# Score stacks filled by SBUF-to-SBUF transfers, partner transfers issued by GpSimd

## The chip, the cores and the metric

The kernel runs on one core of a Trainium2 chip. The time is device microseconds of one execution; 924.72 us is the median of 3 runs (924.64 to 926.47).

## The reference

One layer of two blocks over x of [16, 128, 512] (batch, channel, time). The first is cross-attention over channels as rows: x is normalised over its last axis, q = Wq x + bq from it, k and v from the context, 8 heads of 16 channels, the first 8 channels of each head of q and k rotated (rotary embedding), then softmax(q k / 4) v over 512 x 512 scores per head, an output projection, and a gated sum. The second is a feed-forward block with fp4 weights.

```python
q = _proj(Wq, bq, layernorm(x)); k = _proj(Wk, bk, ctx); v = _proj(Wv, bv, ctx)
q, k = _rope(q, 8), _rope(k, 8)        # x_rope * cos + neg_half * sin on channels 0..7 of a head
p_attn = softmax(einsum('bhqd,bhkd->bhqk', q, k) / sqrt(16))
x = x + tanh(g_xattn) * _proj(Wo, bo, einsum('bhqk,bhkd->bhqd', p_attn, v))
x = x + tanh(g_ffn) * ffn(layernorm(x))
```

## The kernel before

`attend` computes the attention, `feed_forward` the second block; only the first is touched. Attention runs as 16 steps, one per batch, each of 16 slots, written out for each engine; engines meet only through semaphores, and each engine's work, SyncE's DMA issues included, is done in the order written.

In slot s of step b TensorE computes (`tensor_step`, L458): scores of batch b+1 (`score`, L412), from which VectorE takes row maxima (`maxima`, L666); scores of batch b once more, transposed, with the maxima subtracted by two more rows of the product (`weigh`, L424), which ScalarE exponentiates (L536); and the product with v for the slots before (`values`, L435). Scores have two PSUM banks, transposed results three.

The score products read *stacks*: for four pairs of heads, rows 0..47 and 64..111 hold a head's 16 channels three times, as head (rounded float32r) and rest (the remainder), in the orders head, head, rest for q and head, rest, head for k, so that one product of 48 rows gives a near-float32 result. In q's stack rows 48, 49 and 112, 113 hold the negated maxima (again head and rest), in k's ones. q and k have two stacks each, for even and odd batches.

How a stack comes about, for batch n = b+3 in step b: two projection calls (`project_rot` at slot 2, `project_pass` at slot 5), each for the q and the k of half the channels; ScalarE adds the bias; SyncE moves the rotary partners with four transfers inside SBUF (`swap_partners`, L216); GpSimd rotates (L596 to L601) and makes rests (L607, L613); VectorE casts heads (L649, L655); SyncE stores heads and rests to `image` in DRAM (L224 to L235, eight transfers of 128 or 256 KB a batch), and in the next steps loads them back into the stacks (`load_half`, L237, eight transfers of 192 KB to 48 partitions).

The maxima of a half of the slots are turned by VectorE (`turn_max`, L673), stored to DRAM (`store_max`, L249) and loaded as rows of the stack (`load_max`, L254). The weighing of slots 0 and 8 waits for them (L428). SyncE's order of a step is `sync_step` (L292), VectorE's `vector_step` (L710), GpSimd's `pool_step` (L783). Sums of exponentials are gathered (L261), halves merged (L268), inverted on VectorE at slot 6 (L684), and go through DRAM (L274, L279).

Of the kernel before, what the change touches and what calls it, by code (L numbers as in the profile page):

```python
# [17 lines left out]
P = 128  # L18
# [29 lines left out]
X_TILES, C_TILES, PROBS = 8, 4, 3  # L48
MIX_AT, ROT_AT, PASS_AT, V_AT = 1, 2, 5, 8
AHEAD_PROJ = 3  # L50

IMG_ROWS, K_ROW0 = 102, 49
STEP_ROWS = 6
# [12 lines left out]
def transposed_items():  # L66
    items = []
    for n in range(AHEAD_PROJ):
        items += [("rot", n), ("pass", n)]
    for b in range(B):  # L70
        for slot in range(SLOTS):
            items += [("weight", b, 2 * slot), ("weight", b, 2 * slot + 1)]
            if slot == MIX_AT and b >= 2:
                items.append(("mix", b - 2))
            if slot == ROT_AT and b + AHEAD_PROJ < B:
                items.append(("rot", b + AHEAD_PROJ))
            if slot == PASS_AT and b + AHEAD_PROJ < B:
                items.append(("pass", b + AHEAD_PROJ))
    items += [("mix", B - 2), ("mix", B - 1)]
    return items  # L80
# [16 lines left out]
def attend(nc, d, keep):  # L97
    with ExitStack() as ctx:
# [4 lines left out]
        halves = (slice(0, P // 2), slice(P // 2, P))  # L103
# [4 lines left out]
        scale = sb("qk_scale", [P, 1], F32)  # L108
# [12 lines left out]
        swap, turned = sb("swap", [P, T], F32), sb("turned", [P, T], F32)  # L121
        split_head = sb("split_head", [P, 2, T], F32R)
        split_rest = sb("split_rest", [P, 2, T], F32R)

        q_stack = [sb(f"q_stack{p}", [P, PAIRS, T], F32R) for p in two]
        k_stack = [sb(f"k_stack{p}", [P, PAIRS, T], F32R) for p in two]
        v_ones = [sb(f"v_ones{p}", [P, KT, QUAD, QUADS, 2 * KC], F32) for p in two]
# [29 lines left out]
        ones_set = sem("ones_set")  # L157
        gated = sem("gated")
# [17 lines left out]
        pass_head = sem("pass_head")  # L176
        pass_rest = sem("pass_rest")
        rot_head = sem("rot_head")
        rot_rest = sem("rot_rest")
        stored = [sem(f"stored_{w}") for w in ("rot", "pass")]  # L180
        half_in = [[sem(f"half_in{p}{h}") for h in two] for p in two]
# [4 lines left out]
        max_in = [[sem(f"max_in{p}{h}") for h in two] for p in two]  # L186
# [12 lines left out]
        PARTS = 16 * 4  # L199
        HALF = 16 * 4  # L200
# [3 lines left out]
        image, max_dram, inv_dram = keep["image"], keep["max_dram"], keep["inv_dram"]  # L204

        with nc.Block() as block:
# [9 lines left out]
            def swap_partners(sp, n):  # L216
                sp.wait_ge(st_read, ST_NO["rot", n] + 1)
                if n:
                    sp.wait_ge(rot_rest, n)
                for at in range(0, P, 64):  # L220
                    for to, source in ((at, at + 32), (at + 32, at)):
                        sp.dma_start(swap[to:to + 32, :], proj[source:source + 32, 0, :]).then_inc(swapped, 16)

            def store_head(sp, n, w):  # L224
                sp.wait_ge((rot_head, pass_head)[w], n + 1)
                rows = lambda first, count: image[n, first:first + STEP_ROWS * count:STEP_ROWS].rearrange("r h t -> r (h t)")
                tile = split_head[:, w, :].bitcast(F32)
                sp.dma_start(rows(3 * w + 1, 16), tile).then_inc(stored[w], 16)
                sp.dma_start(rows(3 * w, 8), tile[halves[0]]).then_inc(stored[w], 16)
                sp.dma_start(rows(K_ROW0 + 3 * w + 2, 8), tile[halves[1]]).then_inc(stored[w], 16)  # L230

            def store_rest(sp, n, w):
                sp.wait_ge((rot_rest, pass_rest)[w], n + 1)
                rows = image[n, 3 * w + 2:3 * w + 2 + STEP_ROWS * 16:STEP_ROWS].rearrange("r h t -> r (h t)")
                sp.dma_start(rows, split_rest[:, w, :].bitcast(F32)).then_inc(stored[w], 16)  # L235

            def load_half(sp, n, h):  # L237
                p = n % 2
                for w in two:
                    sp.wait_ge(stored[w], PARTS * (n + 1))  # L240
                if n >= 2:
                    sp.wait_ge(st_full, last_weight(n - 2, h))
                for stack, row0 in ((q_stack, 0), (k_stack, K_ROW0)):
                    for odd in two:
                        rows = stack[p][STACK * odd:STACK * odd + DATA_ROWS, columns(h), :].bitcast(F32)
                        heads = slice(odd * PAIRS + 2 * h, odd * PAIRS + 2 * h + 2)
                        sp.dma_start(rows, image[n, row0:row0 + DATA_ROWS, heads, :]).then_inc(half_in[p][h], 16)
# [6 lines left out]
            def load_max(sp, n, h):  # L254
                sp.wait_ge(max_out[h], 16 * (n + 1))
                for odd in two:
                    row = STACK * odd + DATA_ROWS
                    sp.dma_start(q_stack[n % 2][row:row + MAX_ROWS, columns(h), :].bitcast(F32).rearrange("r j t -> r (j t)"),
                                 max_dram[n, h, :, odd].rearrange("r i e -> r (i e)")).then_inc(max_in[n % 2][h], 16)

            def gather_sums(sp, b, h):  # L261
                sp.wait_ge(pv_out[h], b + 1)
                if b:
                    sp.wait_ge(inverse_out, 16 * QUADS * b)
                first = KC if h == 0 else 0
                sp.dma_start(sums[64 * h:64 * h + 64, :], pv_sb[h][b % 2][first:P:2 * KC, :]).then_inc(sums_in[h], 16)

            def merge_quads(sp, b):  # L268
                sp.wait_ge(sums_in[0], 16 * (b + 1))
                for j in range(QUAD):  # L270
                    rows = slice(2 * KC * j + KC, 2 * KC * (j + 1))
                    sp.dma_start(pv_sb[0][b % 2][rows, :], pv_sb[1][b % 2][rows, :]).then_inc(merged[b % 2], 16)

            def store_inverse(sp, b):  # L274
                sp.wait_ge(inverses, b + 1)
                for h in two:
                    sp.dma_start(inv_dram[b, :, h, :], sums[64 * h:64 * h + 64, :]).then_inc(inverse_out, 16)

            def load_inverse(sp, b):  # L279
                sp.wait_ge(inverse_out, 16 * QUADS * (b + 1))  # L280
                if b:
                    sp.wait_ge(heads_ok, b)
                sp.dma_start(scale_of[:], inv_dram[b].rearrange("j h t -> (j h) t").unsqueeze(1).to_broadcast(
                    [HEADS, KC, T])).then_inc(inverse_in, 16)
# [7 lines left out]
            def sync_step(sp, b):  # L292
                nxt, proj_n = b + 1 < B, b + AHEAD_PROJ
                if nxt:
                    load_half(sp, b + 1, 1)
                store_max(sp, b, 1)
                if proj_n < B:
                    swap_partners(sp, proj_n)
                if b:
                    gather_sums(sp, b - 1, 1)  # L300
                    merge_quads(sp, b - 1)
                load_max(sp, b, 1)
                if b >= 2:
                    store_x(sp, b - 2)
                if b:
                    store_inverse(sp, b - 1)
                if proj_n < B:
                    store_head(sp, proj_n, 1)
                if b + 2 < B:
                    load_half(sp, b + 2, 0)  # L310
# [4 lines left out]
                if proj_n < B:  # L315
                    store_rest(sp, proj_n, 1)
                if b + 5 < B:
                    load_inputs(sp, b + 5)
# [906 lines left out]
```

## Time and profile before

| | us |
|---|---|
| median of 3 runs | 924.72 |
| the profiled execution's own time | 918.37 |
| its span | 916.6 |
| TensorE busy | 815.8 |
| VectorE busy | 522.1 |
| ScalarE busy | 483.6 |
| GpSimd busy | 178.5 |

The span runs from the first to the last instruction of the profiled execution; its own time is 1.8 us longer, and it was 6.35 us faster than the median. Attention takes the span up to about 485 us, the feed-forward block the rest. A busy share is an average over both. PEclk is the clock that TensorE was granted, as a share of 2.4 GHz.

### The profile page before, as it was taken

What the parts mean: (1) busy time and instruction counts of PE and PEld (TensorE: products, weight loads), DVE (VectorE), ACT (ScalarE), POOL (GpSimd) and SP (SyncE); (2) the same over time, 40 slices, a digit from 0 to 9 for tenths busy, and PEclk for the clock granted to TensorE, in tenths of its full rate; (3) what the DMA queues carried; (4) which work ended last, traced back from release to release, by engine and by line L of the source; (5) the groups of instructions that cost most, each with busy time, mean ns of one, the idle gap of its engine ahead of it and who ended that gap; (6) DMA issues with size and microseconds to landing.
All of it is one profiled execution on the core that took longest, in us unless ns stands there. A gap on an engine that the chain in (4) does not pass through costs nothing. (4 is left out here: it accounts for less than half of the span.)

```text
span 916.6 us, 13653 instructions
## 1 busy us (share of the span) xinstructions
PE 815.8 (89%) x5110; PEld 421.6 (46%) x5142; DVE 522.1 (57%) x760; ACT 483.6 (53%) x895; POOL 178.5 (19%) x174
## 2 busy tenths in 40 slices
PE   3378999999998988999993599999999999999997
PEld 1123333333333333334332376666666666666664
DVE  4398977888987867888871961314131423141113
ACT  2227776887787766778792552325231623252223
POOL 1232333333333423331112820000000000000000
PEclk8559999999999988999996889999999999999999
DMA  5678555666665666465212010002000110000001
GB/s 167 171 198 218 155 142 153 189 200 194 170 165 152 175 175 189 119 167 153 69 33 79 8 46 1 1 1 67 25 1 1 47 45 0 0 27 21 0 1 46
DMA packets 55176, 86.44 MB, mean 94 GB/s; under 512 B 19274, under 2 KB 20938, under 8 KB 55114
## 3 DMA queue, kind: packets, MB, share of 16 engines
q1 hardware_dynamic: 55114, 85.62, 33.0%
q8 instruction: 38, 0.62, 0.3%
q14 instruction: 24, 0.20, 0.1%
HBM read 44.70 MB, written 34.34 MB: 86 GB/s over the span
## 5 line engine op out<-in xcount | busy, mean ns | idle before, releaser
L670 DVE TENSOR_REDUCE neg_max<-s_ps 128x2 f32<-128x1024 f32 x256 | 310.0, 1219 | 61.8 <-PE s_ps L420 60.8
L536 ACT ACTIVATE probs<-st_ps 128x512 f32<-128x512 f32 x512 | 277.9, 597 | 105.5 <-PE st_ps L432 101.2
L448 PE MATMUL pv_ps<-probs,v_ones 128*32 128x256 f32 x2048 | 166.1, 397 | 12.6 <-ACT pv_sb L542 12.6
L1098 PE MATMUL gu_ps<-x_head,gu_head 128*128 128x512 f32 x352 | 155.9, 443 | 0.0
L965 DVE TENSOR_TENSOR hidden<-gu_ps,silu 128x512 f32<-128x512 f32 x44 | 30.4, 691 | 202.6 <-ACT silu L1040 202.6
L420 PE MATMUL s_ps<-k_stack,q_stack 48*128 48x512 f32 x512 | 135.4, 526 | 10.5 <-DVE neg_max L670 8.4
L1099 PE MATMUL gu_ps<-x_rest,gu_head 128*128 128x512 f32 x352 | 139.0, 395 | 0.0
L1040 ACT ACTIVATE silu<-gu_ps 128x512 f32<-128x512 f32 x44 | 26.3, 597 | 204.8 <-PE gu_ps L1101 204.8
L432 PE MATMUL st_ps<-q_stack,k_stack 50*128 50x512 f32 x512 | 110.6, 421 | 12.9 <-DMA q_stack<-max_scratch 12.7
L420 PEld LDWEIGHTS s_ps<-k_stack,q_stack 48*128 48x128 f32 x512 | 50.4, 193 | 121.1 <-issue 81.1
L1115 PE MATMUL y_ps<-dn_head,h_head 128*128 128x512 f32 x176 | 101.5, 577 | 1.1 <-DVE h_rest L967 1.0
L448 PEld LDWEIGHTS pv_ps<-probs,v_ones 128*32 128x32 f32 x2048 | 41.6, 108 | 115.2 <-ACT probs L536 94.0
L1101 PE MATMUL gu_ps<-x_bf,gu_rest 128*128 128x512 bf16 x333 | 87.4, 381 | 1.2
L1098 PEld LDWEIGHTS gu_ps<-x_head,gu_head 128*128 128x128 f32 x352 | 66.8, 190 | 17.7
L432 PEld LDWEIGHTS st_ps<-q_stack,k_stack 50*128 50x128 f32 x512 | 61.6, 191 | 24.8 <-DMA q_stack<-max_scratch 16.5
L1099 PEld LDWEIGHTS gu_ps<-x_rest,gu_head 128*128 128x128 f32 x352 | 66.3, 188 | 14.3
L1115 PE MATMUL y_ps<-dn_head,h_rest 128*128 128x512 f32 x176 | 68.4, 389 | 0.0
L1115 PE MATMUL y_ps<-dn_rest,h_bf 128*128 128x512 bf16 x163 | 63.5, 390 | 0.0
L967 DVE TENSOR_TENSOR h_rest<-hidden,h_head 128x512 fp32r<-128x512 f32 x44 | 30.5, 692 | 30.8 <-ACT h_head L1046 30.8
L1101 PEld LDWEIGHTS gu_ps<-x_bf,gu_rest 128*128 128x128 bf16 x352 | 27.4, 98 | 44.7 <-issue 24.1
L1046 ACT ACTIVATE h_head<-hidden 128x512 fp32r<-128x512 f32 x44 | 27.8, 632 | 35.3 <-DVE hidden L965 35.3
L1115 PEld LDWEIGHTS y_ps<-dn_rest,h_bf 128*128 128x128 bf16 x176 | 16.9, 96 | 47.0 <-issue 47.0
(114 smaller groups left out, 807.1 us busy)
## 6 DMA issues: line engine op xcount, KB each, us to landing
q_stack<-image SPq DMA_DIRECT2D x64, 192.0 KB, 3.9
k_stack<-image SPq DMA_DIRECT2D x64, 192.0 KB, 4.5
image<-split_head SPq DMA_DIRECT2D x32, 256.0 KB
image<-split_head SPq DMA_DIRECT2D x64, 128.0 KB
image<-split_rest SPq DMA_DIRECT2D x32, 256.0 KB
ct<-ctx_dram SPq DMA_DIRECT2D x16, 256.0 KB, 5.5
swap<-proj SPq DMA_DIRECT2D x64, 64.0 KB, 2.0
scale_of<-inverse_scratch SPq DMA_DIRECT2D x16, 256.0 KB
```

Source lines behind the costliest of these rows:

```text
L420: last = nc.tensor.matmul(out[:, odd, :], q_stack[p][rows, j, qt * P:(qt + 1) * P], k_stack[p][rows, j, :], start=True, stop=True)
L432: nc.tensor.matmul(out[:], k_stack[p][rows, j, kt * P:(kt + 1) * P], q_stack[p][rows, j, :], start=True, stop=True).then_inc(st_full, 1)
L448: last = nc.tensor.matmul(pv_ps[2 * KC * j:2 * KC * (j + 1), cols], v_ones[b % 2][:, kt, j, quad, :], probs[at % PROBS][:, j, cols], start ...
L536: nc.scalar.activation(probs[at % PROBS][:, tile % 4, :], st_ps[item % ST_BANKS][:], ACT.Exp).then_inc(st_read, 1)
L670: nc.vector.tensor_reduce(neg_max[j // 2][:, :, j % 2, qt], s_ps[item % S_BANKS][:], AXIS_X, ALU.max, negate=True).then_inc(s_read, 1)
L965: nc.vector.tensor_tensor(hidden[t % 2][:], gu_ps[t % 2][:, 1], silu[t % 2][:], ALU.mult).then_inc(hid_ok, 1)
L967: nc.vector.tensor_tensor(h_rest[t % 2][:], hidden[t % 2][:], h_head[t % 2][:].bitcast(F32), ALU.subtract).then_inc(h_rests, 1)
L1046: nc.scalar.activation(h_head[t % 2][:], hidden[t % 2][:], ACT.Copy).then_inc(h_heads, 1)
L1098: nc.tensor.matmul(gu_ps[t % 2][:, half], head, x_head[:, k], start=(k == 0), stop=False)
L1099: nc.tensor.matmul(gu_ps[t % 2][:, half], head, x_rest[:, k], start=False, stop=False)
L1101: last = nc.tensor.matmul(gu_ps[t % 2][:, half], keep["gu_rest"][:, k, col:col + P], x_bf16[:, k], start=False, stop=(k == KT - 1))
L1115: last = nc.tensor.matmul(y_ps[:, j, :], h[t % 2][:, cols], keep[w][:, t, :], start=(t == 0 and n == 0), stop=(t == IT - 1 and n == 2))
```

## The change

The DRAM image goes. A projection call now makes all of q or all of k of a batch (slots 9 and 12); the channels are ordered by (odd head, channel, pair) in each, so that a whole tile of 128 rows is one side of all heads. Rotation works on whole tiles of q and k together, 128 x 1024, with cosine 1 and sine 0 for channels that are not rotated; VectorE casts both heads at once (slot 4), one pass makes both rests. Six transfers inside SBUF fill a stack: 64 rows by 2 KB twice go to 16 rows of 16 KB. q and k share a stack tile, and there are three. The partner transfers move only rotated rows and are issued by GpSimd (`swap_partners` in `pool_step`). Merge, inverse store and v's layout change so that each is one transfer. The order of SyncE's step is new.

```diff
-MIX_AT, ROT_AT, PASS_AT, V_AT = 1, 2, 5, 8
+MIX_AT, HEADS_AT, V_AT, Q_AT, K_AT = 1, 4, 5, 9, 12
+BLOCKS = ((Q_HEAD, K_HEAD), (Q_HEAD, K_REST), (Q_REST, K_HEAD))
...
+            def swap_partners(pool, n):
+                pool.wait_ge(st_read, ST_NO["k", n] + 1)
                 if n:
+                    pool.wait_ge(rotated, n)
+                block = QUAD * ROT // 2
+                for odd in two:
+                    low = STACK * odd
+                    for to, source in ((low, low + block), (low + block, low)):
+                        pool.dma_start(swap[to:to + block], proj[source:source + block]).then_inc(swapped, 16)
+            def fill_stacks(sp, n, blocks):
+                stack = stacks[n % STACKS]
+                for at in blocks:
+                    q, k = BLOCKS[at]
                     for odd in two:
+                        rows = stack[STACK * odd + KC * at:STACK * odd + KC * (at + 1)].bitcast(F32)
+                        pair = split[STACK * odd:STACK * (odd + 1), q:k + 1:k - q, :].bitcast(F32)
+                        sp.dma_start(rows.rearrange("c j w t -> c (j w t)"), pair).then_inc(stack_in[n % STACKS], 16)
+            def build_stacks(sp, n):
+                if n >= STACKS:
+                    sp.wait_ge(st_full, last_weight(n - STACKS, 1))
+                sp.wait_ge(heads, n + 1)
+                fill_stacks(sp, n, (0,))
+                sp.wait_ge(rests, n + 1)
+                fill_stacks(sp, n, (1, 2))
...
             def sync_step(sp, b):
+                nxt = b + 1 < B
                 store_max(sp, b, 1)
                 if b:
                     gather_sums(sp, b - 1, 1)
+                load_max(sp, b, 1)
+                if b:
                     merge_quads(sp, b - 1)
                     store_inverse(sp, b - 1)
+                if b + 2 < B:
+                    build_stacks(sp, b + 2)
                 if nxt:
                     store_max(sp, b + 1, 0)
                 if b:
                     load_inverse(sp, b - 1)
+                if b + 4 < B:
+                    load_inputs(sp, b + 4)
                 if nxt:
                     load_max(sp, b + 1, 0)
+                if b >= 2:
+                    store_x(sp, b - 2)
                 gather_sums(sp, b, 0)
...
             def _(sp):
...
+                sp.wait_ge(ones_set, STACKS)
+                build_stacks(sp, 0)
                 load_inputs(sp, 3)
+                build_stacks(sp, 1)
                 store_max(sp, 0, 0)
                 load_max(sp, 0, 0)
...
             def score(pe, n, slot):
+                p = n % STACKS
+                if slot == 0:
+                    pe.wait_ge(stack_in[p], STACK_LOADS * stack_turn(n))
...
+            def bias_projection(act, n, which):
...
                 if n:
+                    act.wait_ge(rests, n)
...
+            def by_cosine(engine, ops, n):
+                engine.wait_ge(st_read, ST_NO["k", n] + 1)
+                ops.tensor_tensor(turned[:], proj[:], both(cos), ALU.mult).then_inc(cosine, 1)
+            def by_sine(engine, ops, n):
+                engine.wait_ge(swapped, SWAPS * (n + 1))
+                ops.tensor_tensor(swap[:], swap[:], both(sin), ALU.mult).then_inc(sine, 1)
+                engine.wait_ge(cosine, n + 1)
+                engine.wait_ge(sine, n + 1)
+                ops.tensor_tensor(proj[:], swap[:], turned[:], ALU.add).then_inc(rotated, 1)
+            def split_rests(engine, ops, n):
+                engine.wait_ge(heads, n + 1)
+                ops.tensor_tensor(split[:, Q_REST:K_REST + 1:K_REST - Q_REST, :], proj[:],
+                                  split[:, Q_HEAD:K_HEAD + 1, :].bitcast(F32), ALU.subtract).then_inc(rests, 1)
...
+                    if slot == HEADS_AT and b + 2 < B:
+                        split_heads(dve, b + 2)
...
             def pool_step(pool, b):
+                if b + 2 < B:
+                    by_sine(pool, nc.gpsimd, b + 2)
+                if b + AHEAD_PROJ < B:
+                    normalise(pool, nc.gpsimd, b + AHEAD_PROJ)
+                if b + 2 < B:
+                    split_rests(pool, nc.gpsimd, b + 2)
                 if b >= 2:
                     residual(pool, nc.gpsimd, b - 2)
                 if b:
                     scale_heads(pool, nc.gpsimd, b - 1)
+                if b + AHEAD_PROJ < B:
+                    swap_partners(pool, b + AHEAD_PROJ)
+                    by_cosine(pool, nc.gpsimd, b + AHEAD_PROJ)
```

## Rows read from the trace of the kernel before

**Rows 1.** The page: engines' busy time, clock in 40 slices, landing of a partner transfer.

```profile
PE 815.8 (89%) x5110; PEld 421.6 (46%) x5142; DVE 522.1 (57%) x760; ACT 483.6 (53%) x895; POOL 178.5 (19%) x174
...
PEclk8559999999999988999996889999999999999999
...
swap<-proj SPq DMA_DIRECT2D x64, 64.0 KB, 2.0
```

**Rows 2.** Waits by total: engine, waited for, us in total, times, longest.

```profile
PE st_ps L432 <- DMA q_stack<-max_scratch: 12.7, 9, 1.9
...
PE s_ps L420 <- DMA k_stack<-image: 2.0, 1, 2.0
```

**Rows 3.** TensorE's timeline: start, duration, instruction, count, idle before.

```profile
16.43 0.80 PE L408 MATMUL s_ps<-wv,ct 128*128 128x128 f32 x2 [6.01 <-DMA bias_o<-bo_dram]
...
39.36 1.32 PE L420 MATMUL s_ps<-k_stack,q_stack 48*128 48x512 f32 x4
...
60.66 0.66 PE L432 MATMUL st_ps<-q_stack,k_stack 50*128 50x512 f32 x2
...
249.71 0.50 PE L432 MATMUL st_ps<-q_stack,k_stack 50*128 50x512 f32 x2 [1.37 <-DMA q_stack<-max_scratch]
...
253.68 0.64 PE L396 MATMUL st_ps<-xn,wq 128*64 128x512 f32 x1
...
254.69 0.64 PE L448 MATMUL pv_ps<-probs,v_ones 128*32 128x256 f32 x8
...
277.06 0.50 PE L432 MATMUL st_ps<-q_stack,k_stack 50*128 50x512 f32 x2 [1.77 <-DMA q_stack<-max_scratch]
...
331.39 0.79 PE L432 MATMUL st_ps<-q_stack,k_stack 50*128 50x512 f32 x2 [1.93 <-DMA q_stack<-max_scratch]
...
438.98 0.40 PE L432 MATMUL st_ps<-q_stack,k_stack 50*128 50x512 f32 x2
```

**Rows 4.** SyncE's DMA issues in step 7, same columns (five lines of 28).

```profile
255.61 2.49 SPq L222 DMA_DIRECT2D swap<-proj  x4
...
263.17 1.25 SPq L277 DMA_DIRECT2D inverse_scratch<-sums  x2
...
266.36 0.85 SPq L247 DMA_DIRECT2D q_stack<-image  x2
...
268.19 0.53 SPq L252 DMA_DIRECT2D max_scratch<-max_lines  x1
...
273.07 0.55 SPq L258 DMA_DIRECT2D q_stack<-max_scratch  x2
```

**Rows 5.** VectorE's timeline: rotation, reciprocals, a turned maximum; same columns.

```profile
19.27 0.69 DVE L598 TENSOR_TENSOR swap<-swap,sin 128x512 f32<-128x512 f32 x1 [0.65 <-DMA swap<-proj]
...
261.97 0.34 DVE L687 RECIPROCAL sums<-sums 128x32 f32<-128x32 f32 x1
...
263.84 0.21 DVE L682 STREAM_TRANSPOSE max_lines<-max_rows 128x32 f32<-128x32 f32 x1
...
346.48 0.34 DVE L687 RECIPROCAL sums<-sums 128x32 f32<-128x32 f32 x1
```

**Rows 6.** Windows: length, busy of five engines, PEclk, DMA share, GB/s.

```profile
7.00:8.00 1.00, 1.00 (x4) 0.41 (x6) 0.85 (x1) 0.00 (x0) 0.00 (x0) 1.00 1.05 376
28.50:34.50 6.00, 0.00 (x0) 0.00 (x0) 0.00 (x0) 0.00 (x0) 0.00 (x0) 0.50 1.02 230
260.40:260.90 0.50, 0.50 (x4) 0.18 (x4) 0.07 (x1) 0.21 (x1) 0.49 (x1) 1.00 0.36 82
334.00:338.00 4.00, 4.00 (x16) 1.20 (x14) 1.19 (x1) 1.86 (x3) 0.76 (x1) 0.52 0.71 191
95.00:375.00 280.00, 257.89 (x2124) 100.44 (x2124) 229.79 (x295) 210.16 (x395) 97.33 (x81) 0.96 0.61 168
```

**Rows 7.** GpSimd's timeline: one product of 128x512; columns as before.

```profile
261.03 1.28 POOL L601 TENSOR_TENSOR swap<-swap,turned 128x512 f32<-128x512 f32 x1
```

**Rows 8.** ScalarE's timeline: a projection's bias; columns as before.

```profile
254.81 0.78 ACT L518 ACTIVATE proj<-st_ps,qk_bias,qk_scale 128x512 f32<-128x512 f32 x1
```

More of the change, by code:

```diff
@@ L120, in attend @@
         proj = sb("proj", [P, 2, T], F32)
[L121 to L127, printed above, removed]
+        swap, turned = sb("swap", [P, 2, T], F32), sb("turned", [P, 2, T], F32)
+        split = sb("split", [P, 4, T], F32R)
+        stacks = [sb(f"stacks{n}", [P, PAIRS, 2, T], F32R) for n in range(STACKS)]
+        v_ones = [sb(f"v_ones{p}", [P, KT, QUAD, V_WIDTH], F32) for p in two]
         probs = [sb(f"probs{n}", [P, QUAD, T], F32) for n in range(PROBS)]
@@ L157, in attend @@
         ones_set = sem("ones_set")
+        blank = sem("blank")
         gated = sem("gated")
@@ L175, in attend @@
         rotated = sem("rotated")
[L176 to L181, printed above, removed]
+        heads = sem("heads1")
+        rests = sem("rests1")
+        stack_in = [sem(f"stack_in{n}") for n in range(STACKS)]
         max_head = [sem(f"max_head{h}") for h in two]
@@ L185, in attend @@
         max_out = [sem(f"max_out{h}") for h in two]
-        max_in = [[sem(f"max_in{p}{h}") for h in two] for p in two]
+        max_in = [[sem(f"max_in{n}{h}") for h in two] for n in range(STACKS)]
         pv_done = sem("pv_done")
@@ L203, in attend @@
         last_weight = lambda b, quad: ST_NO["weight", b, (quad + 1) * 2 * SLOTS // QUADS - 1] + 1
-        image, max_dram, inv_dram = keep["image"], keep["max_dram"], keep["inv_dram"]
+        max_dram, inv_dram = keep["max_dram"], keep["inv_dram"]
+        both = lambda table: table[:].unsqueeze(1).to_broadcast([P, 2, T])
         with nc.Block() as block:
@@ L224, in store_head @@
[L224 to L230, printed above, removed]
@@ L419, in score @@
                     rows = slice(STACK * odd, STACK * odd + DATA_ROWS)
-                    last = nc.tensor.matmul(out[:, odd, :], q_stack[p][rows, j, qt * P:(qt + 1) * P], k_stack[p][rows, j, :],
+                    last = nc.tensor.matmul(out[:, odd, :], stacks[p][rows, j, 0, qt * P:(qt + 1) * P], stacks[p][rows, j, 1, :],
                                             start=True, stop=True)
@@ L431, in weigh @@
                     out = st_bank(pe, ("weight", b, 2 * slot + odd))
-                    nc.tensor.matmul(out[:], k_stack[p][rows, j, kt * P:(kt + 1) * P], q_stack[p][rows, j, :],
+                    nc.tensor.matmul(out[:], stacks[p][rows, j, 1, kt * P:(kt + 1) * P], stacks[p][rows, j, 0, :],
                                      start=True, stop=True).then_inc(st_full, 1)
@@ L480, in _ @@
                 pe.wait_ge(weights_in, WEIGHTS)
-                project_rot(pe, 0)
-                project_pass(pe, 0)
+                for which in "qk":
+                    project(pe, 0, which)
                 pe.wait_ge(const_in, CONSTS)
@@ L485, in _ @@
                 for n in (1, 2):
-                    project_rot(pe, n)
-                    project_pass(pe, n)
+                    for which in "qk":
+                        project(pe, n, which)
                 pe.wait_ge(scales_f32, 2)
@@ L571, in _ @@
                 nc.scalar.preload_act_table_set("natural_log_exp_and_others")
-                act.wait_ge(consts, 5)
+                act.wait_ge(consts, 2)
                 inverse_dev(act, 0)
-                for n in range(AHEAD_PROJ):
-                    bias_rot(act, n)
-                    bias_pass(act, n)
-                    if n < 2:
-                        inverse_dev(act, n + 1)
+                for n in two:
+                    for which in "qk":
+                        bias_projection(act, n, which)
+                    inverse_dev(act, n + 1)
                 act.wait_ge(scales_in, 32)
```

288 lines of the change are left out of this document (84 added, 204 removed).

## The prediction

> **What bounds the kernel now.** I read the page's engine table and slices first. TensorE is busy for 89% of the span, but its granted clock is low in places: slices 2 and 3 (the start), and slices 15 and 16 [rows 1]. The chain of waits that ended last lies in the feed-forward stage, and the change is all in the attention stage; so I went on to the waits and to timelines of single steps.
>
> The attention stage is 16 steps of 16 slots. TensorE's first weighing of step 0 is at 60.66 us and that of step 14 at 438.98 [rows 3]: (438.98 - 60.66) / 14 = 27.0 us a step. Inside a step TensorE runs without gaps except at one place. At slot 0 the weighing waits for the maximum rows that come back from DRAM (`load_max`): 9 waits, 12.7 us, the longest 1.9 [rows 2]. Step 7 is 277.06 - 249.71 = 27.35 us, of which 1.77 is that wait for step 8 [rows 3]: 25.6 us are TensorE's own. A wait costs more than itself: the one of 1.93 us before 331.39 is followed by a weighing of 0.79 instead of 0.50 us [rows 3] and by a clock of 0.52 in the window from 334 to 338, so almost all of it at 1.2 GHz [rows 6].
>
> Why the maxima come late is seen in the DMA issues of SyncE [rows 4]. The last maximum of the half is turned at 264.05 (263.84 + 0.21, [rows 5]), but the store is issued at 268.19, behind four stack loads from 266.36 on, and has landed only when its load is issued at 273.07: the store lies behind 768 KB of stack loads in one queue. The load is then used at 277.06, 4.0 us later [rows 3, 4]. So the bound of a step is TensorE, with this round trip 1.3 us too late; whatever stands ahead of the maximum store in SyncE's queue moves the end one for one.
>
> **The change part by part.**
>
> TensorE's projections: now q and k go side by side in halves of the array, 253.68 to 254.69 = 1.01 us for each of the two calls [rows 3]. Afterwards a call is one full product of the same 512 columns in the same two records, so the two calls cost what the two pairs did: nothing gained or lost, 0.2 us a step at most. They move from slots 2 and 5 to 9 and 12.
>
> SyncE: a step now issues 38 DMAs (4 partner, 2 + 4 for sums and merge, 2 inverse stores, 8 image stores, 8 stack loads, 10 others); afterwards 21. At about 0.6 us each (4 in 2.49 us, [rows 4]) the queue is relieved by some 10 us a step. SyncE then waits for things, not for its own issue time. By itself this would remove the waits of [rows 2].
>
> VectorE: two casts of 128x512 become one of 128x1024: the same. It is moved to slot 4 and waits for the rotation there; behind it stand the maxima of slot 5, and TensorE has only two score banks. ScalarE has the same number of passes.
>
> GpSimd: products of 128x512 take 1.28 us [rows 7]; a batch has three double ones for the rotation and one for the rest (4 x 2.56), normalise 0.8, residual and scaling 2 x 1.3: 13.6 us, plus four DMA issues. The trace shows no DMA issued by GpSimd. Bounds: 0.6 us each as on SyncE, 1.28 us as one of its own products; I take 0.9, the middle, since nothing is nearer to one end. The chain for batch b+2 begins with its k projection at slot 12 of step b-1, about 19.6 us after the step's start; ScalarE's bias ends 1.9 us behind the start of the product (255.59 against 253.68, [rows 3, 8]), issues take 3.6, the cosine product 2.6, the sine product and the sum 5.1: 32.8, or 7.5 us into a following step of 25.3. The cast of slot 4 comes up at about 7.7. So with steps of 25 us it just fits; with longer ones it has room.
>
> The stack fills are the large item. Stores and loads through DRAM (1.5 MB out, 1.5 MB back a batch) go; in their place are six transfers of 256 KB between places of SBUF, each *to 16 partitions* (`rows` is KC = 16 rows high). What a transfer moves depends in this trace on how many rows it reaches [rows 6]: in the window 7 to 8 us, transfers with 128 rows, 376 GB/s; from 28.5 to 34.5 us, with nothing but stack loads to 48 rows, 230 GB/s, at a DMA share of 1.0 in both. Per busy engine this is 22 against 14 GB/s, so engines share something that depends on the rows. For 16 rows there is only `merge_quads`, 32 KB each: 82 GB/s in the half microsecond of one of them, again 14 GB/s per busy engine (82 / 16 / 0.36), one packet per engine. Bounds for a fill: 230 GB/s (1.14 us, 6.8 a batch) and 82 GB/s (3.2 us, 19.2 a batch). 48 rows instead of 128 cost a factor 1.63; once more from 48 to 16 gives about 135 GB/s, and the one row with 16 partitions says 82. I take 115 GB/s, nearer to the latter in kind: 2.3 us a fill, 13.7 us a batch.
>
> The Trainium skill, in "SBUF — State Buffer", section "Door 1: The DMA port swizzle", says that a transfer's rate follows from how many of 16 SBUF ports its partitions reach, and states 104 GB/s for partitions 0 to 15, 196 for 0 to 63 and 328 for all 128. The trace agrees in the order and roughly in the size (230 and 376). By the page's 104 GB/s a batch's fills would be an estimated 15.1 us, and the time some 20 us above my sum. It speaks against this change, since the fills save bytes but choose the narrowest shape.
>
> Now the path of a step, from its slot 0. SyncE's order is: sums, `store_inverse` (which waits for the reciprocal of VectorE's slot 6), all six fills, and only then the maximum store for the next step. The reciprocal is at 261.97 - 249.71 = 12.3 us in a step at full clock, and at 346.48 - 331.39 = 15.1 in the one that began at the low clock [rows 3, 5]; two projections move out from in front of it and the v projection and a longer cast move in, so I keep both. Plus 0.34 and one issue of 0.65: first fill issued at 13.3 (16.1). From the first stack load's issue to the landing of the maximum store behind it are 273.07 - 266.36 = 6.7 us [rows 4], with 768 KB at 230 GB/s = 3.4 in it: 3.3 fixed. With the fills 3.3 + 13.7 = 17.0. Then 4.0 from the load's issue to the weighing. Period: 13.3 + 17.0 + 4.0 = 34.3 us at full clock, 37.1 where the clock fell. The wait is then 9 us in a step of 25.3 of work, and TensorE stands idle for far longer than the 1.93 us after which the clock was seen low. I count two of three steps with the low clock: 36.2, that is 9.2 more than 27.0.
>
> Fourteen steps fill stacks (b = 0 to 13): 14 x 9.2 = 129, less 3 since step 0 has no reciprocal to wait for: 126.
>
> Start: `const_in` is there at 16.4 (TensorE's v projection starts then, [rows 3]); GpSimd's issues 3.6, landing 2.0 [rows 1], VectorE's rotation 4 x 0.69 [rows 5], cast and rest 2: first fill issued at 26, last landed at 26 + 3.3 + 13.7 = 43; scores now begin at 39.36 [rows 3]. But `store_max(0)` stands behind batch 1's fills: ScalarE's bias of batch 1 waits for the rests (27), swaps issued to 33, landed 35, GpSimd's products to 41, cast at VectorE's slot 6 (near 51), store landed at 51 + 3.3 + 13.7 = 68, load 2 to 4 more: first weighing near 70 against 60.66: plus 9.
>
> Sum against the profiled execution, 918.4 us (span 916.6 and 1.8 around it): 918.4 + 126 + 9 = 1053. The median of the runs shown is 6.3 above that execution, so I forecast 1060. Bounds: at 82 GB/s 5.5 us more a step, 1137; at 150 GB/s and no low clock the period is 31.1, or 14 x 4.1 + 5 = 62: 987.
>
> **The rivals.**
>
> *A, the fills run as wide as the loads did (230 GB/s or more).* Then they take 6.8 us, the maximum store lands at 13.3 + 3.3 + 6.8 = 23.4 and the load 2 to 3 us later, at the end of the 25.3 us of work. The waits go (12.7 + 2.0, [rows 2]) and with them the low clock behind them (mean clock 0.96 from 95 to 375: 280 x 0.04 = 11 us, [rows 6]), less 4 at the start and up to 5 for casts that wait: 924.7 - 17 = 908, range 900 to 918. For it: fewer bytes, SyncE relieved, no DRAM in between. Against it: 14 GB/s per busy engine already with one packet each. It decides from about 8 us of fills a batch (195 GB/s): below that the change is faster.
>
> *B, A's fills, but the partner chain on GpSimd decides.* At 1.28 us an issue or more, the rotated tile is there at 9 or later, VectorE stands at slot 4 for 1.3 to 2.5 us, TensorE loses about 1 us of it in 13 steps: 908 + 13 to 20 = 921 to 928. The Trainium skill ("DMA: Bandwidth & Descriptors", section "SWDGE vs HWDGE vs iDMA") says that such DMAs have their descriptors made by GpSimd's own cores; no row here can show the price, and none of my terms uses it.
>
> *C, the forecast's mechanism without the clock.* Period 34.3: 14 x 7.3 + 9 = 111: 1035. It is inside my range.
>
> **How the numbers follow.** Forecast with C: 0.82. A: 0.12. B 0.04, spread over all three signs. Fills near the point of decision: 0.02. About 0.2% (2 us) is what a measurement of this kernel can tell from no change. Faster 0.13, same 0.02, slower 0.85. The range 985 to 1095 holds the forecast's own spread (150 to 98 GB/s); A and B lie outside it with 0.16, and the end at 82 GB/s with a few hundredths.
>
> **What would show it.** Right: in the DMA part fills of 256 KB take over 8 us to land as the last of six, moving near 115 GB/s at a DMA share near 1.0; TensorE waits 7 to 10 us for `max_scratch` at slot 0 of each step; steps are 33 to 38 us; PEclk is low in every step; SyncE waits for `max_lines` in DRAM. The partner transfers land before GpSimd needs them. Wrong: fills at 200 GB/s or more, steps near 25.5 us and no such wait (A); VectorE's idle time in front of the cast (B).

## The result, and the profile after

The changed kernel takes 1048.4 us (median of 4 runs, 1045.96 to 1050.26), the kernel before 925.6 beside it (924.64 to 931.17): ratio 1.131, 95% interval 1.126 to 1.136. The forecast was 1060 with a range of 985 to 1095. Some executions of a version run 1 to 2% longer at a lower granted clock; the ratios leave them out, and of the traces below that of e10 is of such an execution (1068.07 us). The page after, first TensorE's busy time, granted clock and DMA slices, then two DMA issues with KB and median us to landing:

```profile
PE 848.4 (81%) x5078; PEld 433.1 (41%) x5078; DVE 530.5 (51%) x740; ACT 480.3 (46%) x895; POOL 262.8 (25%) x225
...
PEclk9559888898798889889888978899999999999999
DMA  4686635753674475367435111100020011001001
...
stacks<-split SPq DMA_DIRECT2D x96, 256.0 KB, 8.7
...
swap<-proj POOLq DMA_DIRECT2D x64, 64.0 KB, 2.5
```

Against [rows 1] the busy share of TensorE falls from 89% to 81%, and the clock is below 9 tenths in 17 of the slices 5 to 26, where it was so in 5 of them. Waits by total, after:

```profile
PE s_ps L377 <- DMA stacks<-split: 64.0, 15, 9.8
PE st_ps L389 <- DMA stacks<-max_scratch: 48.6, 14, 4.3
```

The wait for the maxima of [rows 2] has grown from 12.7 to 48.6 us, and one for the stacks has come beside it. TensorE's timeline after, the lines that answer to [rows 3]:

```profile
42.81 1.22 PE L377 MATMUL s_ps<-stacks 48*128 48x512 f32 x4 [9.79 <-DMA stacks<-split]
...
71.86 0.80 PE L389 MATMUL st_ps<-stacks 50*128 50x512 f32 x2 [1.19 <-DMA stacks<-max_scratch]
...
242.72 0.79 PE L389 MATMUL st_ps<-stacks 50*128 50x512 f32 x2 [3.68 <-DMA stacks<-max_scratch]
...
274.36 0.79 PE L377 MATMUL s_ps<-stacks 48*128 48x512 f32 x2 [3.42 <-DMA stacks<-split]
279.15 0.80 PE L389 MATMUL st_ps<-stacks 50*128 50x512 f32 x2 [3.99 <-DMA stacks<-max_scratch]
...
564.40 0.79 PE L389 MATMUL st_ps<-stacks 50*128 50x512 f32 x2 [1.79 <-DMA stacks<-max_scratch]
```

The first weighing is at 71.86 instead of 60.66 (11.2 later); from step 0 to step 14 it is (564.40 - 71.86) / 14 = 35.2 us a step instead of 27.0, which makes 492.5 - 378.3 = 114.2; together 125 of the 127.4 us by which the span grew (1044.0 against 916.6). Step 5 is 279.15 - 242.72 = 36.4 us. SyncE's DMA issues in it, then the windows (columns as in [rows 6]):

```profile
258.31 4.44 SPq L230 DMA_DIRECT2D stacks<-split  x6
262.79 0.56 SPq L243 DMA_DIRECT2D max_scratch<-max_lines  x1
...
274.46 0.56 SPq L249 DMA_DIRECT2D stacks<-max_scratch  x2
```

```profile
262.00:272.00 10.00, 8.42 (x74) 3.09 (x72) 7.36 (x6) 7.60 (x15) 0.00 (x0) 1.00 1.06 112
276.00:279.00 3.00, 0.00 (x0) 0.00 (x0) 0.89 (x4) 0.00 (x0) 1.49 (x2) 0.50 0.44 161
95.00:375.00 280.00, 218.57 (x1635) 84.97 (x1634) 181.88 (x224) 162.95 (x309) 114.37 (x86) 0.85 0.55 84
```

The six fills saturate the 16 DMA engines (share 1.06) at 112 GB/s. The store of the maxima, issued at 262.79, lies behind them, so its load can be issued only at 274.46, and the weighing starts at 279.15. TensorE stands still twice before it, and from 276 to 279 its clock is at the lower of its two levels (0.50).

### The profile page after: what moved, and what is told of

Same layout as the page of the kernel before. It is cut to its first block and busy times, and to the rows that moved or that the text cites. A ratio compares the mean times of both kernels' runs of the same rounds, so it can differ in the third digit from the quotient of the medians.

```text
span 1044.0 us, 13252 instructions
## 1 busy us (share of the span) xinstructions
PE 848.4 (81%) x5078; PEld 433.1 (41%) x5078; DVE 530.5 (51%) x740; ACT 480.3 (46%) x895; POOL 262.8 (25%) x225
## 5 line engine op out<-in xcount | busy, mean ns | idle before, releaser
L377 PE MATMUL s_ps<-stacks 48*128 48x512 f32 x512 | 142.7, 551 | 73.9 <-DMA stacks<-split 64.0
L405 PE MATMUL pv_ps<-probs,v_ones 128*32 128x256 f32 x2048 | 175.1, 416 | 15.4 <-ACT pv_sb L491 15.4
L389 PE MATMUL st_ps<-stacks 50*128 50x512 f32 x512 | 118.9, 450 | 48.6 <-DMA stacks<-max_scratch 48.6
L377 PEld LDWEIGHTS s_ps<-stacks 48*128 48x128 f32 x512 | 53.2, 203 | 190.7 <-issue 84.2
L1028 PE MATMUL gu_ps<-x_bf,gu_rest 128*128 128x512 bf16 x352 | 91.2, 382 | 0.0
L389 PEld LDWEIGHTS st_ps<-stacks 50*128 50x128 f32 x512 | 63.7, 204 | 64.6 <-DMA stacks<-max_scratch 54.9
L571 POOL TENSOR_TENSOR heads_out<-pv_sb,scale_of 128x512 f32<-128x512 f32 x15 | 19.0, 1264 | 282.4 <-DMA scale_of<-inverse_scratch 282.4
L1042 PE MATMUL y_ps<-dn_rest,h_bf 128*128 128x512 bf16 x176 | 68.6, 390 | 0.0
L894 DVE TENSOR_TENSOR h_rest<-hidden,h_head 128x512 fp32r<-128x512 f32 x44 | 30.5, 692 | 30.9 <-ACT h_head L973 30.9
```

The costliest lines, as they stand in the source:

```text
L377: last = nc.tensor.matmul(out[:, odd, :], stacks[p][rows, j, 0, qt * P:(qt + 1) * P], stacks[p][rows, j, 1, :], start=True, stop=True)
L389: nc.tensor.matmul(out[:], stacks[p][rows, j, 1, kt * P:(kt + 1) * P], stacks[p][rows, j, 0, :], start=True, stop=True).then_inc(st_full, 1)
L405: last = nc.tensor.matmul(pv_ps[2 * KC * j:2 * KC * (j + 1), cols], v_ones[b % 2][:, kt, j, 2 * KC * quad:2 * KC * (quad + 1)], probs[at % ...
L894: nc.vector.tensor_tensor(h_rest[t % 2][:], hidden[t % 2][:], h_head[t % 2][:].bitcast(F32), ALU.subtract).then_inc(h_rests, 1)
L1028: last = nc.tensor.matmul(gu_ps[t % 2][:, half], keep["gu_rest"][:, k, col:col + P], x_bf16[:, k], start=False, stop=(k == KT - 1))
L1042: last = nc.tensor.matmul(y_ps[:, j, :], h[t % 2][:, cols], keep[w][:, t, :], start=(t == 0 and n == 0), stop=(t == IT - 1 and n == 2))
```

## The experiments

My theory: the fills' low rate, for their narrow destination, and SyncE's order (six fills ahead of the maxima's store) make all of the loss. Every ratio is to the kernel before on the same chip, whose medians there were 929 to 935 us; the times beside it are medians. In e1, e2, e5, e8, e9 and e10 the stacks do not get the values that they should: the kernel leaves that out and does the rest of the work.

**1. Fills from 128 rows to 128 rows (e1), the likeliest rival to a queue explanation.** Both ends are widened at once.

```diff
-  rows = stack[STACK * odd + KC * at:STACK * odd + KC * (at + 1)]
-  pair = split[STACK * odd:STACK * (odd + 1), q:k + 1:k - q, :]
+  flat = elsewhere[:, 2 * at + odd, :]          # 128 rows of a tile nothing reads
+  sp.dma_start(flat, split[:, (q, k)[odd], :])
```

> The six fills of 256 KB a batch go, from whole tiles of 128 rows, to 128 rows of a tile that nothing reads; the stacks keep the ones they start with, so scores are left out in value though not in work. Theory (the rows reached set the rate): fills move near 376 GB/s as other 128-row transfers did, 0.7 us each and 4 a batch instead of 14.4; no wait for stacks or maxima, steps near 25.5 us, time 900 to 912. Rival (bytes between two places of SBUF cost this much wherever they go): fills stay near 109 GB/s, time 1048.

959.4 us, ratio 1.033 (1.021 to 1.044). The rate is as expected (table below) and both waits for a DMA at slot 0 are gone, but 1.033 x 924.7 = 955 is 47 us above the 908 of rival A. VectorE's timeline, then GpSimd's, at a step's slot 0:

```profile
238.31 3.91 DVE L614 CAST max_rows<-neg_max 128x16 fp32r<-128x16 f32 x1
242.25 0.17 DVE L616 TENSOR_TENSOR max_rows<-neg_max,max_rows 128x16 fp32r<-128x16 f32 x1
```

```profile
237.49 2.38 POOL L545 TENSOR_TENSOR turned<-proj,cos 128x1024 f32<-128x1024 f32 x1
239.82 2.36 POOL L549 TENSOR_TENSOR swap<-swap,sin 128x1024 f32<-128x1024 f32 x1
```

A cast of 16 columns, 0.18 us otherwise, lasts 3.91 us, from inside GpSimd's first double product until its second has ended (242.18). TensorE then waits for VectorE's maxima. This wait in e1, and the same one in the kernel before (total, times, longest):

```profile
PE s_ps L377 <- DVE neg_max L608: 42.6, 39, 3.3
```

```profile
PE s_ps L420 <- DVE neg_max L670: 8.4, 16, 1.3
```

So a second cost lies under the first: the 32 casts of e1 last 44 us longer in all than at 0.175 us each. In the changed kernel itself it hardly shows (same cast: median 0.175 us, longest 2.02), because there the cast comes at another moment of GpSimd's chain: in step 5 at 240.23, when the double products begin only at 244.35.

**2. The same with GpSimd's products in quarters (e5).**

```diff
-  ops.tensor_tensor(turned[:], proj[:], both(cos), ALU.mult)
+  for c in cuts:                                # four of 128 columns; so too L549, L552, L556
+      ops.tensor_tensor(turned[:, :, c], proj[:, :, c], both_of(cos, c), ALU.mult)
```

> The wide fills of e1_wide (to 128 rows of an unused tile, so scores are left out in value), and GpSimd's four double products are cut into quarters of 128 columns each, same work. Theory: in e1_wide VectorE's 128x16 cast of the maxima took up to 4.8 us instead of 0.17 because it stood behind whole GpSimd products of 2.4 us; with quarters of 0.6 us it takes at most about 1.2, steps come from 31 to 26 us, time 1.5 to 5% below e1_wide (905 to 940 where the kernel before has 925). Rival (the cast waits for something else, or the step is long for another reason): casts still near 4 us, time as e1_wide.

944.2 us, ratio 1.018 (1.009 to 1.027); the interval overlaps that of e1, so a gain of some 1.5% over e1 is likely and not certain, and 944 lies above the 905 to 940 expected. The block did not go away; VectorE's timeline, and GpSimd's:

```profile
230.83 0.52 DVE L619 CAST max_rows<-neg_max 128x16 fp32r<-128x16 f32 x1
231.39 3.37 DVE L621 TENSOR_TENSOR max_rows<-neg_max,max_rows 128x16 fp32r<-128x16 f32 x1
```

```profile
229.85 2.80 POOL L547 TENSOR_TENSOR turned<-proj,cos 128x256 f32<-128x256 f32 x4
232.62 2.79 POOL L552 TENSOR_TENSOR swap<-swap,sin 128x256 f32<-128x256 f32 x4
```

Between two quarters of 0.7 us VectorE mostly does not get its turn: the cast or the small product behind it still waits up to 3.4 us, over several of them. It became less, though: over all 32 pairs of cast and small product the time beyond 0.175 us each is 44 us in e1 and 30 us in e5, and TensorE's wait for VectorE 42.6 and 30.9. Shorter instructions help by a third and don't open the gap. The granted clock falls after such a block too: in e5 one of 3.20 us begins at 386.26, TensorE then stands for 2.13 us (before 391.55) and 0.46 us (before 393.69), and the window from 394 on is

```profile
394.00:402.00 8.00, 8.00 (x44) 3.65 (x42) 5.26 (x6) 2.60 (x5) 4.70 (x6) 0.50 0.05 19
```

**3. Half the columns (e2)**

```diff
-  rows = stack[...];                pair = split[..., q:k + 1:k - q, :]
+  rows = stack[..., :, :, 0:T // 2]; pair = split[..., q:k + 1:k - q, 0:T // 2]
```

> Each fill moves only the first 256 of 512 columns (128 KB instead of 256), still to 16 rows; the other columns of the stacks keep ones, so scores are left out in value. Theory (109 GB/s for 16 rows, in front of the maximum store): 7.2 us less a batch and the wait at slot 0 shrinks from 8 us to 1 or none, with part of the low clock: steps of 26 to 29 us, time 905 to 950. Rival (a fixed cost per transfer, or SyncE's wait for the reciprocal, makes the step long): less than 20 us gained, 1030 or more.

977.0 us, ratio 1.052 (1.039 to 1.065). Halving the bytes takes 1048 to 977, and the wait for the maxima is left at 8.2 us in all (48.6 in the change). That is short of the 905 to 950 expected: the blocked cast is back (up to 5.95 us), with 40.6 us of waits for VectorE's maxima against 9.9 in the change. That these make up the whole rest is argued, not shown.

**4. The fills on two queues (e3), and all on GpSimd's (e4)**

```diff
 # e3: SyncE keeps the even half's three fills, GpSimd issues the odd half's; e4: GpSimd issues all six
-  build_stacks(sp, b + 2)
+  pool_heads(pool, b + 2); split_rests(...); pool_rests(pool, b + 2)
```

> The three fills of the odd half (rows 64 to 111) are issued by GpSimd on its own queue, the three of the even half by SyncE, all bytes and rows as before. Theory in its port form (two groups of 16 rows, 0 to 63 and 64 to 127, don't share what limits the rate): both queues move at once, together near 200 GB/s, fills take 7 to 8 us, time 905 to 950. Rival (the 16 DMA engines themselves are slow on such transfers, whatever stands beside): together still 109 GB/s, but the maximum store waits only behind SyncE's half: 1000 to 1048.

1007.2 us, ratio 1.082 (1.069 to 1.094).

> All six fills are issued by GpSimd after its own work, so SyncE's queue holds no fills; rate and rows as before. Theory that the place in the queue is half of the loss: the maximum store passes beside the fills, fills start 2 to 4 us earlier since they don't stand behind the inverse store; the step is bounded by fills of 14.4 us from 12 us on, 27 to 29 us a step, time 915 to 950. Rival (the rate alone decides, other transfers crawl beside fills on the same 16 DMA engines): steps of 33 us or more, 1000 or more.

1008.9 us, ratio 1.088 (1.074 to 1.103). The windows of e3, then of e4, while fills run:

```profile
252.00:254.00 2.00, 1.56 (x12) 0.34 (x12) 1.93 (x5) 1.53 (x3) 0.16 (x1) 1.00 1.07 127
254.00:256.00 2.00, 1.79 (x16) 0.64 (x15) 2.00 (x3) 1.41 (x3) 0.00 (x0) 1.00 1.07 122
```

```profile
254.00:258.00 4.00, 3.48 (x30) 1.31 (x26) 3.22 (x3) 3.50 (x8) 0.00 (x0) 1.00 1.05 111
258.00:262.00 4.00, 4.00 (x44) 1.51 (x36) 3.08 (x3) 3.16 (x6) 0.00 (x0) 1.00 1.07 137
```

Two queues side by side move some 125 GB/s where one moves 112: the same 16 engines are full (share 1.07). The gain is not shown to be the second queue's: e4, with all fills in one, moves 111 and 137 (the latter with SyncE's loads of x and ctx beside them). In e4 no fill stands in SyncE's queue ahead of the maxima, and still the store issued at 250.95 had its load issued only at 259.89, and the weighing waits 1.9 to 4.9 us in most steps, 42.4 us in all: small transfers crawl beside the fills too, not only behind them. So the prediction's picture of a store that waits *behind* the fills in SyncE's queue was only half of it. Both gain 40 us on the change; the likely reason, argued only, is that fills on GpSimd's queue start without waiting for the reciprocal (246.07 in e4).

**5. SyncE's order (e6, e11).**

```diff
   build_stacks(sp, b + 2)                       # now the heads' two fills only
+  store_inverse(sp, b - 1)
   store_max(sp, b + 1, 0)
+  load_max(sp, b + 1, 0)                        # e11 only; e6 leaves it behind load_inputs
+  fill_rests(sp, b + 2)                         # the other four
   load_inverse(sp, b - 1); load_inputs(sp, b + 4)
```

> Only SyncE's order differs from the changed kernel: the two fills of the heads are issued before the inverse store, and the maximum store for the next step before the four fills of the rests. Theory (rate and place together make the step long): the heads' fills run in a stretch where the queue was empty, the maximum store waits behind at most two of six fills, step 36.4 becomes 29 to 32 us, time 955 to 1000. Rival (the rate alone decides): 1030 or more. If no fill stood in the way at all it would be below 930.

1025.0 us, ratio 1.106 (1.097 to 1.116): a miss. TensorE in e6:

```profile
265.96 0.50 PE L384 MATMUL s_ps<-stacks 48*128 48x512 f32 x2 [0.82 <-DMA stacks<-split]
270.68 0.80 PE L396 MATMUL st_ps<-stacks 50*128 50x512 f32 x2 [4.21 <-DMA stacks<-max_scratch]
```

The store now goes early (253.81), but the load is issued at 259.49 behind four fills and the inputs and is used 11 us later. So e11 moved the load as well:

> The changed kernel with the maxima taken wholly out of the fills' shadow: two fills for the heads, store and load of the maxima, then the four fills for the rests, then the inverse and the inputs. With the earlier reordering the load stood behind four fills and the inputs and TensorE still waited 4.2 us for it in each of 14 steps, beside 0.8 us for the stacks. Queue-place theory: the 4.2 us go, the rests' fills start about 2 us later (SyncE waits for the store to land), so 2 us come back as a wait for the stacks: steps of 34.0 - 2.2 = 31.8, 1025 - 31 = 994 us, range 975 to 1005. If the fills' own 13.7 us decide whatever the order (rival): the wait for the stacks takes all 4 us, 1020 to 1030 us.

1036.6 us, ratio 1.113 (1.101 to 1.125), no better than e6 and far from the 975 to 1005 expected. Its wait for the maxima is gone (1.1 us once); in its place stand 2.8 to 3.6 us for the stacks, and 1.0 to 2.2 us in which the output projection waits for GpSimd's scaled heads (18.1 us in all, 9 times), in the steps of 33 to 34 us around here; its steps 2 to 13 take 35.1 us on average. GpSimd's timeline of e11 shows what paces these steps, with SyncE's issues of the same step:

```profile
242.16 1.26 POOL L577 TENSOR_TENSOR heads_out<-pv_sb,scale_of 128x512 f32<-128x512 f32 x1 [18.29 <-DMA scale_of<-inverse_scratch]
243.36 2.00 POOL L221 DMA_DIRECT2D swap<-proj  x4
...
250.22 2.36 POOL L558 TENSOR_TENSOR proj<-swap,turned 128x1024 f32<-128x1024 f32 x1
...
275.29 1.27 POOL L577 TENSOR_TENSOR heads_out<-pv_sb,scale_of 128x512 f32<-128x512 f32 x1 [17.85 <-DMA scale_of<-inverse_scratch]
```

```profile
253.38 1.24 SPq L230 DMA_DIRECT2D stacks<-split  x2
...
263.81 1.40 SPq L274 DMA_DIRECT2D scale_of<-inverse_scratch  x2
```

A ring: the load of `scale_of` (263.81) lies behind the fills and lands at 275.29; GpSimd, in its order, issues the partner transfers only after the scaling that needs it; three double products and the cast (285.76 to 286.45) follow; the next batch's fills are issued at 286.53, 33.15 us after the last ones (10.4 + 11.5 + 11.2). I had not seen this ring: the partner transfers were put on an engine whose queue waits for a transfer behind the fills. In e6 it is nearly closed too, but not quite: the rotation ends at 279.44 and the cast comes at 281.81, in its place in VectorE's order. That breaking the ring would free the step was not tried.

**6. The partner transfers back on SyncE, the fills as they are (e12).**

```diff
   store_max(sp, b, 1)
+  swap_partners(sp, b + 2)
-  swap_partners(pool, b + AHEAD_PROJ)
```

> The changed kernel with only the partner transfers put back on SyncE, behind its store of the maxima of heads 1 (where the kernel before had them), the fills as they are. My steps say that the fills wait for the reciprocal (14.8 us into the step) and not for the rotation (11.5 us), so which engine issues the partner transfers costs nothing: 1040 to 1056 us, same. Rival: the 2 us that GpSimd spends on issuing stand on the path through cast and fills: 1015 to 1030 us. Other rival: SyncE now waits for the key projection with the gathers behind it, so the reciprocal comes later: 1060 to 1080 us.

1051.2 us, ratio 1.133 (1.125 to 1.142), beside 1.131 for the whole change: who issues them costs nothing measurable here, since the fills wait for the reciprocal (257.49 in the changed kernel) and not for the cast (ended 254.26). It is a test of the engine and not of the moment: SyncE issued them at 242.88, GpSimd in the change at 242.34.

**7. What sets the fills' rate (e8, e9, e10).**

```diff
 # e8: as the change, but 32 rows of 8 KB of a tile nothing reads
+  flat = elsewhere[32 * (f % 4):32 * (f % 4 + 1), f // 4, :]     # f = 2 * at + odd
 # e9: 64 rows read as in the change, 128 rows of 2 KB written (nothing reads them)
+  sp.dma_start(elsewhere[:, 2 * at + odd, :], split[STACK * odd:STACK * (odd + 1), q:k + 1:k - q, :])
 # e10: 128 rows read, the change's 16 rows of 16 KB written
+  sp.dma_start(rows, split[:, (q, k)[odd], :])
```

> The fills' sources, bytes (256 KB each, 64 source rows) and number as in the changed kernel, but each goes to 32 rows of 8 KB of an unused tile instead of 16 rows of 16 KB; scores are left out in value. Theory (rows reached set the rate): about 200 GB/s, 1.3 us a fill, time near e2_half, 950 to 985. Rival (the reading side or two places in SBUF set it): 109 GB/s and 1040.

1033.0 us, ratio 1.114 (1.103 to 1.126).

> The six fills of a batch read the same 64 rows (two blocks) as the change does, in the same 2 KB pieces, but write 128 rows of a tile that nothing reads (so the scores are those of stale rows); the widened fills before them read 128 rows and wrote 128. Theory W (the written rows set the rate): 2.5 us a fill as with the widened fills, 955 to 965 us in all. Theory R (the rows read set it, since going from 16 to 32 rows written moved the rate only from about 112 to 123 GB/s): 115 to 125 GB/s, 1020 to 1050 us. If both ends have a share: about 200 GB/s (64 rows read), 960 to 985 us.

975.0 us, ratio 1.056 (1.047 to 1.066).

> The mirror: each fill reads one block of all 128 rows and writes the same 16 rows of 16 KB of the stack as in the change (the scores are then of other numbers). Theory W: nothing is won, 1040 to 1055 us at 105 to 120 GB/s. Theory R: 2.5 us a fill, 955 to 970 us. Both ends: 1040 to 1055, as the narrower end decides.

1051.7 us, ratio 1.135 (1.127 to 1.143). One window with fills alone in each of e1, e8, e9 and e10:

```profile
256.50:259.50 3.00, 3.00 (x24) 1.00 (x16) 2.10 (x5) 1.68 (x4) 0.00 (x0) 0.61 1.02 375
```

```profile
256.00:264.00 8.00, 7.48 (x67) 2.83 (x65) 6.28 (x6) 6.47 (x12) 0.00 (x0) 1.00 1.05 123
```

```profile
256.50:260.50 4.00, 3.73 (x28) 1.27 (x26) 3.46 (x4) 3.31 (x8) 0.00 (x0) 1.00 0.98 252
```

```profile
266.00:274.00 8.00, 7.49 (x68) 2.85 (x66) 6.29 (x6) 6.47 (x12) 0.00 (x0) 1.00 1.09 114
```

| | rows read | rows written, run in each | GB/s, engines full | us |
|---|---|---|---|---|
| change | 64 | 16 x 16 KB | 112 | 1048 |
| e10 | 128 | 16 x 16 KB | 114 | 1052 |
| e8 | 64 | 32 x 8 KB | 123 | 1033 |
| e9 | 64 | 128 x 2 KB | 252 | 975 |
| e1 | 128 | 128 x 2 KB | 375 | 959 |

Beside the first line, e10 clears the reading side: with a narrow destination it makes no difference whether 64 or 128 rows are read. e9 shows that the written side is worth a factor 2.2 by itself, and e1 that once it is wide, the read side is worth another 1.5. That the *number* of rows does it is not shown: twice the rows (e8) brought 10%, where some 200 GB/s had been expected. In the table rows and the length of the run in a row change together, but e2 separates them: it writes 16 rows too, in eight separate runs of 1 KB each instead of one of 16 KB, and its fills move 116 and 120 GB/s. The first of these windows:

```profile
265.00:267.00 2.00, 2.00 (x21) 0.61 (x20) 1.46 (x2) 1.46 (x3) 0.00 (x0) 1.00 1.17 116
```

So neither the long run nor the size of a packet makes it slow: the trace has packets of 1 KB in e2's fills and of 2 KB in most of the others' (the page of e2 counts 12288 more under 2 KB, 128 for each of its 96 fills), and a packet of 2 KB takes 0.31 us in the change and in e10, 0.30 in e8, 0.12 in e9 and 0.09 in e1 (medians in these windows). Left are the number of rows and how many pieces in a row go to the same one (eight in the change and in e2, four in e8, one in e9 and e1); which of them it is stays open.

The Trainium skill ("SBUF — State Buffer", section "Door 1: The DMA port swizzle") gives 104 GB/s for partitions 0 to 15, 189 for 0 to 31 and 328 for all 128. The trace agrees for 16 (112) and roughly for 128 (375); for 32 rows filled with runs of 8 KB it does not: 123 was measured, and that decides.

**8. A version that beats both (e7).** The same lesson put to the kernel before, whose maxima's store lay behind four stack loads [rows 4]:

```diff
+  store_max(sp, b + 1, 0)
   load_half(sp, b + 2, 0)
-  store_max(sp, b + 1, 0)
   load_inverse(sp, b - 1)
+  load_max(sp, b + 1, 0)
   store_rest(...); load_inputs(sp, b + 5)
-  load_max(sp, b + 1, 0)
```

> The kernel before, with the store of the next step's maxima issued ahead of the four stack loads, and their load ahead of the rest store and the input loads. Theory (what stands ahead of the maxima in SyncE's queue moves the end one for one): the 9 waits of 12.7 us in all go and most of the low clock behind them, 900 to 915 where the kernel before has 925. Rival (the waits are the latency of the two DRAM transfers, or the stack loads become late instead): 920 to 930.

901.6 us, ratio 0.973 (0.965 to 0.981): faster than both. SyncE's issues:

```profile
244.87 0.53 SPq L252 DMA_DIRECT2D max_scratch<-max_lines  x1
245.51 0.86 SPq L247 DMA_DIRECT2D q_stack<-image  x2
246.42 0.89 SPq L247 DMA_DIRECT2D k_stack<-image  x2
...
248.20 0.61 SPq L258 DMA_DIRECT2D q_stack<-max_scratch  x2
```

From the store's issue to the load's it is now 3.3 us (248.20 - 244.87), where it was 273.07 - 268.19 = 4.9 [rows 4] after 1.8 us behind the loads, and of the 12.7 us of [rows 2] TensorE still waits 4.5, although this trace is of e7's longest execution (913.26); its waits have

```profile
PE st_ps L432 <- DMA q_stack<-max_scratch: 4.5, 5, 1.5
```

## Why the prediction was right, step by step

- *(Fill rate.)* 115 GB/s taken, 112 measured at a share of 1.06. The bounds were wide (82 to 230), and the choice (nearest row in kind) held; that it came so close is in part luck. The reason given, rows reached, is only partly borne out; e8 contradicts it as a rule by row count. (The factor 1.63 applied to 230 gives 141, not the "about 135" written there; 115 lies between that and 82 either way.)
- *(Path of a step.)* First fill issued 15.6 us after slot 0 (16.1 at the low clock); first fill to the load of the maxima 274.46 - 258.31 = 16.15 (17.0); load to weighing 4.7 (4.0). Sum 36.4 in step 5, against 37.1 at the low clock: three terms off by under 1 us, partly cancelling. The 36.2 of the forecast took the low clock in two of three steps; it came in every one from 135.42 on, and that error and the terms' own made each other good.
- *(Form of the wait.)* Not 9 us in one place: 3.4 us at the next score, for the stacks (a wait that the prediction did not have), and 4.0 at the weighing, 7.4 in all. The other 29.0 us of the step are TensorE's work, which was 25.6: the 3.4 more go with the low clock after the waits (mean 0.85 instead of 0.96 from 95 to 375). I had counted the wait too long and the work too short.
- *(Start.)* First scores at 42.8 (43 forecast), first weighing 71.9 (70), so +11.2 against +9. The first fill was issued at 24.98, where 26 was written (the terms there add up to 26.8). The second batch's path was not the one told: its partner transfers, issued at 27.80 beside the first fills, landed at 42.90 and not after 2 us, so that GpSimd stood for 10.7 us, against the sign that they land before it needs them. The cast came at 51.58 all the same (51 forecast), so the end is right in part by luck.
- *(14 steps.)* 114 against 126: 36.2 was the step of the middle (ten steps from 135.42 to 495.42: 36.0 each), but step 0 takes 98.51 - 71.86 = 26.7, where 3 us less than the others had been counted, and the last two 34.5. Of the 11 us that 14 x 36.2 - 3 is too long, 6.5 are step 0's. This term, and the 6.3 added for the median of the runs shown (the changed kernel's median is 2.4 above its traced execution), make the forecast too high.
- *(GpSimd.)* An issue costs 1.99 / 4 = 0.50 us (0.9 taken, 0.6 the lower bound: measured below it), a double product 2.36 (2.56). The partners are not issued when the projection is ready but at slot 0, after the scaling: the prediction's chain for GpSimd missed what is queued in front of them. In the change this cost nothing (the cast ended 3.6 us before the reciprocal on which the fills wait had ended, 257.83); in e11 it sets the step.
- *(Rival A)* priced fast fills at 908. e1 had them and took 959: "up to 5 us for casts that wait" was mis-sized about ninefold (44 us of blocked casts), and the clock that falls after such waits comes on top. *Rival B* (921 to 928) was nearer in kind for e1, GpSimd's chain deciding, but through blocked casts, not through a late rotation.
- *(Low clock as a surcharge)* is seen in every step from 135.42 on, whose first weighing takes 0.79 or 0.80 us, where one at 2.4 GHz takes 0.50 (249.71 in [rows 3]); rival C (1035) without it was too low.

What stays open: whether the number of rows or the pieces that follow each other into one row set the write rate, and what is won by e11 with its ring cut.

## What to carry to other kernels

Before bytes are saved by going SBUF to SBUF, look at the shape at the written end: a good quarter fewer bytes (61 instead of 86 MB) took 13% longer, since they went at 112 GB/s to 16 rows. A small transfer on which TensorE waits must be issued ahead of the large ones, and its load too; measured on the kernel before, this alone gave 2.7% (1.9 to 3.5). And when a wait is predicted to vanish, ask what the freed engines then do at the same time: here casts met GpSimd's products.

## What the runs showed of the hardware

- A VectorE cast of 128x16 lasts 0.18 us alone and up to 4.81 (e1), 5.80 (e9) and 5.95 us (e2) beside back-to-back GpSimd products of 2.36 us; it may stay blocked over the boundary between two of them, and a small product with two SBUF inputs as well (3.37 in e5, 5.92 in e9). The Trainium skill ("SBUF — State Buffer", section "Who interferes with whom") says that VectorE's casts can use a port pair that it shares with GpSimd, its instructions with two SBUF inputs meet GpSimd's reads, and whoever issues first holds the pair for its whole instruction. The trace agrees and shows more, that the wait can span several.
- Four DMAs issued by GpSimd take 1.99 us of it; their landing (median 2.5 us) is about that of the same four from SyncE (2.0 in [rows 1], 2.3 in e12); beside narrow fills it took 15 us (issued 27.80, waited for until 42.90, in the changed kernel).
- Narrow fills keep all 16 DMA engines busy at 112 GB/s in one queue and at 122 to 127 in two (shares 1.06 and 1.07); packets of 1 KB (e2, 116 and 120) go no slower than those of 2 KB (112).
